# Binarised convolution on one core: products into an unused bank, planes released one by one, row sums moved

## What is computed

```
v  = group_norm(x, 32 groups)                # per image and group of 8 channels
xn = batch_norm(v) * gamma + beta            # statistics over all images
t  = +1 where xn > 0, -1 otherwise           # sign
xc = clip(xn, -1, 1)
y  = conv3x3(t, conv_w) + conv_b             # 256 -> 256 channels, pad 1
b_sum = conv3x3_of_ones(sum over channels of xc * t) + beta_b
b_cnt = conv3x3_of_ones(256)                         + beta_b
out = x + y * (b_sum / b_cnt)
```

## Time and profile before

| | |
|---|---|
| median of 3 runs | 935.04 us (934.71 to 936.57) |
| the profiled execution, its own time | 934.54 us |
| its span, first to last instruction | 932.7 us |
| PE busy | 782.7 us (84%) |
| DVE busy | 779.0 us (84%) |
| ACT busy | 600.6 us (64%) |
| mean granted TensorE clock | 0.931 of full |

### The profile page before, as it was taken

One profiled execution on the slowest core, in us unless ns is written; L12 is line 12 of the kernel. 1 busy time (PEld: TensorE's weight loads), 2 busy tenths in 40 slices (PEclk: granted clock), 3 DMA queues, 4 the chain that ended last, 5 costly groups with the idle time before them and its releaser, 6 DMA issues. The chain is left out here.

```text
span 932.7 us, 12739 instructions
## 1 busy us (share of the span) xinstructions
PE 782.7 (84%) x4686; PEld 464.9 (50%) x4686; DVE 779.0 (84%) x1217; ACT 600.6 (64%) x490; POOL 141.4 (15%) x160
## 2 busy tenths in 40 slices
PE   2100005999999999999999999999999999999996
PEld 2100003555555555555555555555555555555553
DVE  4999888899888888888888979797879787979755
ACT  2042636868777777777777777777768686868310
POOL 0089400011111111111011111111111111101011
PEclk9655556999999999999999999999999999999998
DMA  9999972369888888888887869696969696958489
GB/s 358 430 405 379 419 325 81 135 180 286 256 243 229 250 227 248 229 237 248 220 266 202 288 174 315 166 316 159 312 168 303 172 291 188 290 157 215 131 214 269
DMA packets 43478, 232.79 MB, mean 250 GB/s; under 512 B 10560, under 2 KB 10688, under 8 KB 39360
## 3 DMA queue, kind: packets, MB, share of 16 engines
q0 software_dynamic: 18144, 101.16, 42.1%
q1 hardware_dynamic: 24544, 131.25, 38.7%
q10 hardware_dynamic: 768, 0.12, 0.1%
HBM read 180.73 MB, written 51.79 MB: 249 GB/s over the span
## 5 line engine op out<-in xcount | busy, mean ns | idle before, releaser
L606 PE MATMUL acc<-V,U 128*128 128x385 f16 (+1 forms) x4608 | 769.4, 330 | 11.8 <-DVE V L832 10.1
L606 PEld LDWEIGHTS acc<-V,U 128*128 128x128 f16 x4608 | 451.0, 98 | 325.6 <-issue 12.8
L477 ACT ACTIVATE sn<-acc,inv_s 128x784 f32<-128x784 f32 x128 | 116.9, 913 | 206.8 <-PE acc L606 200.9
L350 POOL DMA_DIRECT2D y<-x x63 | 53.9, 856 | 724.6 <-DVE y L919 711.4
L919 DVE SCALAR_TENSOR_TENSOR y<-y,vec,bmap 128x1568 f32<-128x1568 f32 (+1 forms) x65 | 117.6, 1810 | 0.2
L455 ACT ACTIVATE r<-xb,ab 128x1568 f32<-128x1568 f32 x64 | 106.6, 1690 | 6.3 <-ACT u L430 4.0
L430 ACT ACTIVATE u<-xb,ab 128x1624 f16<-128x1624 f32 x63 | 109.0, 1732 | 0.2
L440 ACT ACTIVATE T<-u 128x1680 f16<-128x1680 f16 x60 | 95.6, 1594 | 2.2 <-DVE D L826 2.2
L443 ACT ACTIVATE T<-T 128x1568 f16<-128x1568 f16 x58 | 87.6, 1511 | 1.8
L579 PE MATMUL csum<-mv,cst 128*128 128x32 f32 x2 | 0.6, 397 | 90.7 <-DVE mv L690 90.7
L826 DVE TENSOR_TENSOR D<-T 128x1568 f16<-128x1568 f16 x63 | 61.3, 973 | 15.3 <-ACT T L443 15.0
(11 more groups left out here) (110 smaller groups left out, 414.8 us busy)
## 6 DMA issues: line engine op xcount, KB each, us to landing
xb<-x SPq DMA_DIRECT2D x64, 812.0 KB, 6.5
y<-x POOLq DMA_DIRECT2D x63, 784.0 KB, 8.0
out<-y POOLq DMA_DIRECT2D x63, 784.0 KB, 9.3
y<-x SPq DMA_DIRECT2D x16, 1568.0 KB, 8.7
bmap<-map_rows SPq DMA_DIRECT2D x32, 784.0 KB, 6.4
xb<-x SPq DMA_DIRECT2D x14, 1568.0 KB, 10.2
V<-w_t SPq DMA_DIRECT2D x2, 1152.0 KB, 14.7
out<-y SPq DMA_DIRECT2D x2, 392.0 KB, 3.0
```

Source lines behind the costliest of these rows:

```text
L477: nc.scalar.activation(sn[:, b, half], acc[:, b, :, 0:N], ACT.Copy, scale=inv_s[:, b:b + 1])\
L606: last = nc.tensor.matmul(by_row(acc[:, g % 2, bank, 0:N])[:, :, lo:hi], U[:, ci, digits, k, dx, co * P:(co + 1) * P], by_row(V[:, a, ci, ...
```

## The change

Six edits:

1. PE: after the group sums, 36 matmuls of 128 x 392 into `box` (`keep_busy`): 26 as soon as `w_pool` and `scale_ready` allow, 10 after the wait for the coefficients.
2. DVE: groups 0 and 1 of image 0 go through `first_group`: each of the two FIRST planes is made as soon as its half of D is there, the odd one first, as an instruction of 392 elements with its own `v_first`.
3. PE: FIRST of group (0, 0) waits per plane and part (`v_first` 1 to 4), bank 1 first.
4. ACT makes the `T` of group 1 (into `T01`, memory of `y`) after `sign(0, 0, 1)`; DVE made it before. `snapshot(0, 0, 0)` now stands ahead of `sign(0, 0, 3)`, and `snapshot(0, 0, 1)` ahead of `complement(0, 1)`.
5. SP: image 0 uses the usual order, so `crow_load(0)` stands ahead of all loads of image 2.
6. DVE: `beta_map(1)` moves behind `finish(0, 2)`.

The core of the diff:

```diff
+WARM = (26, 10)
+        early = y[:, 0:2].rearrange("p g f -> p (g f)").bitcast(F16).rearrange("p (r w) -> p r w", w=W)
+        T01 = early[:, 0:66]
...
             for g in range(G4):
                 first_load(g)
-            load(0, x_rows[2], 0)
-            load(0, x_rows[2], 1)
             sp.wait_ge(zeros_in, 16)
-            crow_load(0)
-            map_store(0)
-            map_load(0, 0)
-            map_load(0, 1)
-            load(0, x_rows[2], 2)
-            load(0, x_rows[2], 3)
+            image(0, x_rows[2])
...
             sign(0, 0, 1)
+            act.wait_ge(u_ready, 1)
+            act.wait_ge(t_ready, 1)
+            nc.scalar.activation(T01[:, 30:60], u[:, 1, 0:HR + 2], ACT.Relu, scale=2.0).then_inc(t_ready, 1)
             sign(0, 0, 2)
             absolute(0, 0, 0)
             absolute(0, 0, 1)
             complement(0, 0)
+            snapshot(0, 0, 0)
             sign(0, 0, 3)
-            snapshot(0, 0, 0)
             absolute(0, 0, 2)
             absolute(0, 0, 3)
+            snapshot(0, 0, 1)
             complement(0, 1)
-            snapshot(0, 0, 1)
...
+            def keep_busy(count):
+                for _ in range(count):
+                    nc.tensor.matmul(box[:, 0:N], U[:, 0, 0, 0, 0, 0:P],
+                                     U[:, 0, 0, 0].rearrange("p b o -> p (b o)")[:, 0:N], start=True, stop=True)
+            pe.wait_ge(w_pool, WP * CT)
+            pe.wait_ge(scale_ready, 2)
+            keep_busy(WARM[0])
...
                 for part in range(CT if by_channels else 1):
-                    if by_channels:
-                        pe.wait_ge(v_first, part + 1)
-                    for bank in banks:
+                    for bank in banks[::-1] if by_channels else banks:
                         k = planes[bank]
+                        if by_channels:
+                            pe.wait_ge(v_first, 2 * part + 2 - bank)
...
-            pe.wait_ge(w_pool, WP * CT)
+            keep_busy(WARM[1])
             first(0, 0, 0, by_channels=True)
...
+            def first_group(g, t, d):
+                at_least(dve, cq_done, g)
...
+                dve.wait_ge(t_ready, g + 1)
+                nc.vector.tensor_scalar(t[:, 1:28:2], t[:, 31:58:2], 2.0, None, ALU.mult).then_inc(t4_ready, 1)
+                dve.wait_ge(t4_ready, g + 1)
+                nc.vector.tensor_tensor(rows(d[:, 1], 1), pair(3), pair(1), ALU.subtract).then_inc(aq_done, 1)
+                dve.wait_ge(aq_done, g + 1)
+                nc.vector.tensor_tensor(plane(1), d[:, 1, 2:HR:4], d[:, 1, 1:HR:4], ALU.add).then_inc(v_first, 1)
+                nc.vector.tensor_scalar(T8[:, :], t[:, 30:30 + HR], 4.0, 3.0, ALU.mult, ALU.subtract)\
+                  .then_inc(t8_ready, 1)
+                dve.wait_ge(t8_ready, g + 1)
+                nc.vector.tensor_tensor(d[:, 0], t[:, 32:32 + HR], T8[:, :], ALU.subtract).then_inc(cq_done, 1)
+                dve.wait_ge(cq_done, g + 1)
+                nc.vector.tensor_tensor(plane(0), d[:, 0, 2:HR:4], d[:, 0, 1:HR:4], ALU.add).then_inc(v_first, 1)
...
-            differences(0, 0, D00)
-            first_planes(0, 0, 0, D00).then_inc(v_first, 1)
-            differences(0, 1, D)
-            first_planes(0, 0, 1, D).then_inc(v_first, 1)
+            first_group(0, T, D00)
+            first_group(1, T01, D)
...
-            beta_map(1)
...
-            def proceed(n, a):
+            def proceed(n, a, map_after=False):
...
                     finish(*before(g, 3))
+                    if map_after and g == 1:
+                        beta_map(n)
...
-            proceed(1, 1)
+            proceed(1, 1, map_after=True)
```

More of the change, by code:

```diff
@@ L804, in v_planes @@
                 return V[:, a, g % 2, first:first + step + 1:step, g // 2].rearrange("p k (q w) -> p k q w", w=W)
+            def first_group(g, t, d):
+                at_least(dve, cq_done, g)
+                pair = lambda at: t[:, at:at + 62].rearrange("p (j r) w -> p j r w", j=2)[:, :, 0:28:4]
+                plane = lambda j: V[:, 0, g, 2 + 2 * j, 0].rearrange("p (q w) -> p q w", w=W)
+                if g == 0:
+                    dve.wait_ge(u0_ready, 1)
+                    nc.vector.tensor_scalar(t[:, 30:60], u[:, 0, 0:HR + 2], 0.0, 2.0, ALU.max, ALU.mult)\
+                      .then_inc(t_ready, 1)
+                dve.wait_ge(t_ready, g + 1)
[10 more added lines that the diff above has]
+                nc.vector.tensor_tensor(plane(0), d[:, 0, 2:HR:4], d[:, 0, 1:HR:4], ALU.add).then_inc(v_first, 1)
             def differences(m, g, d):
@@ L811, in differences @@
                 if isinstance(m, int) and m == 0:
[L812 to L815, removed]
+                    dve.wait_ge(u_ready, s)
                     nc.vector.tensor_scalar(T[:, 30:60], u[:, g % 2, h:h + HR + 2], 0.0, 2.0, ALU.max, ALU.mult)\
```

## The result

| | before | changed | ratio |
|---|---|---|---|
| median of 11 runs each | 934.71 us (933.60 to 936.92) | 932.50 us (931.67 to 933.17) | 0.9973, 95% interval 0.9965 to 0.9981 |
| the profiled execution | 934.54 us, span 932.7 | 932.56 us, span 930.4 | |

What follows compares the result with a forecast made beforehand. PE bounds the loop, its restart at 223.83 set by the later of PE's and DVE's chains. PE's 0.90 - 0.2 + 0.66 + 0.56 = 1.9 us off 934.54 gives 932.6, plus 0.50 for the median 933.1; range 932.5 to 933.8, chance 0.58.

Steps and rivals of the forecast that it cites:

- DVE's chain: DVE from `beta_map(0)` on: no 2.80 us wait for the row sums, so 2.7 us (2.4 to 3.1) earlier.
- PE's chain: PE from its first product to the restart at 223.83: 1.9 us earlier, the smaller of the two chains.
- the 0.2% line: Least difference told from no change, 1.87 us, so 933.17 is the bound; faster 0.47, same 0.47.
- The 0.50 that I added for the median: Median of the runs taken as 0.50 above the profiled execution, giving 933.1 from 932.6.
- The 24 products: PE's first 24 products in image 0: done at 157.05 instead of 157.95, so PE is 0.90 us ahead.
- The new wait for `ends` of (0, 0): PE ahead of FIRST of group (0, 2), near 173: gives back 0.2 us (0 to 0.4).
- The two old waits: PE's stops at 202.70 (for a `fold`) and 223.83 (`ends` of (1, 0)): both gone, 0.66 + 0.56 us gained.
- Sum on PE: PE's gain at the restart after 223.83: 0.90 - 0.2 + 0.66 + 0.56 = 1.9 us.
- The end: PE's last wait, 1.0 us at the very end; the forecast sum has no term for it.
- The 36 matmuls: PE from 142.40, ahead of the first products: lift the clock after 2.9 us, end at 149.8, cost nothing.
- the broken start: Rival: clock falls among PE's 18 products from 149.8 to 156.05; gain about 0.6, 934.4; chance 0.13.
- DVE stayed late: Rival: small store stays slow or DVE's gain is lost, restart at 223.83 stays; 935.0, in part 934; chance 0.15.

Runs made afterwards that it cites:

- front_only: Edits 1 to 4 alone: the changed kernel with the order of the row sums and of beta_map(1) put back; median 933.80 us, ratio to before 0.9973 to 0.9993.
- rows_only: The kernel before with only the new order of the row sums and of beta_map(1) (edits 5 and 6); median 934.17 us, ratio 0.9983 to 1.0.
- warm_rows: The kernel before with edits 1, 5 and 6 (36 matmuls, new order), planes and T as before; median 933.09 us, ratio 0.9969 to 0.9987.
- before_again: The kernel before, unchanged, run once for a second trace; no median, product 408 at 77.03 us from the start of stage 2 against 76.23 in the first trace.

## Why the store lands sooner: left open

In both traces of before a 16 KB fetch of PE's instructions (0.96 and 1.16 us on a transfer queue of its own) falls at 34.8 or 35.3 us from the start of stage 2, among the two loads and the store; in front_only the 36 matmuls move it to 26.7. Small matmuls in stage 1, where PE is idle, move the fetches alone:

```diff
             last.then_inc(scale_ready, 1)
+            for _ in range(36):
+                nc.tensor.matmul(csum[:, 100:101], mxb[0:1, 0:P], one[:, :], start=True, stop=True)
```

> The kernel before with 36 matmuls of one element in stage 1, where PE is idle for 90 us, into an unused column. They cost no time and do not touch the clock at the first products; they move PE's instruction stream on by 36 matmuls, so each 16 KB fetch comes 6 us earlier, the one at 34.8 us behind the start of stage 2 at about 28.8, ahead of the two loads. Theory (the fetch on the same transfer engines is what made the store of the row sums land 1 us later): the store lands 6.0 us after its issue instead of 7.0, PE restarts at product 408 1.0 us earlier, time 933.9. Rival (the fetch has nothing to do with it): 7.0 us and 934.9.

> front_only with 80 matmuls of one element in stage 1, as in before_shift. The fetches then fall at about 13.4 and 35.4 us behind the start of stage 2, the second of them between the two loads and the store again. Theory (the fetch): the store lands 7.0 us after its issue, restart at 76.0 to 76.3 us, time 934.8, no gain against before, although PE starts 1.5 us earlier. Rival (edits 2 to 4 bring the 1 us): 6.0 us and 933.8.

> front_only with 36 matmuls of one element in stage 1, as in before_shift. One fetch of PE's instructions then falls at about 35 us behind the start of stage 2, between the two loads and the landing of the row sums (31.5 to 38.6 in before). Theory (the fetch costs the store 1 us, and DVE's chain sets PE's restart): the store lands 6.9 to 7.0 us after its issue, restart at product 408 at 76.0 to 76.3 us, time 934.8, so no gain against before, although PE starts 1.5 us earlier. Rival (edits 2 to 4 bring the 1 us): 5.8 to 6.0 us, restart at 75.0 to 75.3, 933.5.

before_shift had its fetches at 20.3 and 41.2, a store of 5.82 us and a restart at 75.22, as the theory says. Its median was 933.73, 1.5 below the 935.23 of before on the same chip, but with one run of 940.2 the interval is 0.9979 to 1.0009, so this is not told from no change. front_shift missed its aim: with 80 the fetches fell at 20.8 and 41.1, so it is one more trace without a fetch beside the store (5.75 us; median 933.38). front_fetch put one at 34.9, and the store landed after 5.06 us:

```profile
179.59 0.40 SPq L231 DMA_DIRECT2D sum_rows<-cs  x1
184.66 0.33 SPq L235 DMA_DIRECT2D crow<-sum_rows  x1
```

Its median was 933.59, like front_only. So a fetch at that time does not always cost the store 1 us, and the theory as I put it falls. I had overlooked, though, that the traces with the new order speak for a part of it: the store took 1.38 to 1.40 us in the nine with no fetch beside it, but 2.55 in rows_only and 2.18 in no_warm, the two where a fetch fell next to it (33.4 against a store issued at 33.0, and 31.4 against 31.5). SP in no_warm:

```profile
178.70 0.40 SPq L231 DMA_DIRECT2D sum_rows<-cs  x1
180.89 0.33 SPq L235 DMA_DIRECT2D crow<-sum_rows  x1
```

The store of image 1 shows no such cost: 3.25 us in no_warm with a fetch beside it, 3.28 in the changed kernel without. What makes the store land sooner is open.

## The clock, the planes, the T

**no_warm** (`WARM = (0, 0)`) and **warm_long** (`WARM = (26, 30)`):

> The changed kernel without the 36 matmuls into the unused bank. The first products begin at about 151.0 us at the half clock. Theory: DVE delivers the four parts 1.9, 1.3 and 1.9 us apart, and six products at the half clock take 1.96, so the half clock is mostly hidden in pauses; what is lost is the part that still lies behind 156.0 us, when the last six begin: 0 to 1 us, depending on when the level rises. I expect it 0 to 0.9 us slower than the changed kernel, so 932.5 to 933.4. Rival (the clock is what the change gains): slower by the 1.5 us that 9 products at the half clock cost, or more, 934.0.

> The changed kernel with 20 more matmuls into the unused bank behind the coefficients (26 and 30 instead of 26 and 10). They take 20 x 0.166 = 3.3 us at the full clock and end at about 154.2 us, past the first three planes, so the 24 first products end at about 158.2 instead of 157.0. Theory (PE's chain is the later one by now): 1.2 us later there, less the wait of 0.2 us at product 120 that it covers, so 1.0 us slower than the changed kernel, 933.5. Rival (DVE's chain still decides): no change against the changed kernel.

Without the 36 matmuls the median is 0.6 higher, 933.08, in the expected range. In its trace the half clock lasted until 155.65, and product 24 was only 0.45 later, since PE's pauses for DVE hid the rest; the runs spread over 3.5 us instead of 1.5. With 20 more: no change (932.43), where I expected 1.0. In the trace the extra matmuls held PE until 152.63 and the 24 products then ran without one pause (PE):

```profile
141.07 11.73 PE L589 MATMUL box<-U 128*128 128x392 f16 x56
152.63 24.08 PE L615 MATMUL acc<-V,U 128*128 128x392 f16 x144
```

Product 24 came 0.7 us later from the start of stage 2 than in the changed kernel, 4583 0.5 later. That is the theory's direction at half the size; the medians of 7 and 11 runs do not show it, so the expected 1.0 was a miss.

**t_on_vector**, the second T made by DVE and not by ACT:

```diff
+                else:
+                    dve.wait_ge(u_ready, g)
+                    nc.vector.tensor_scalar(t[:, 30:60], u[:, 1, 0:HR + 2], 0.0, 2.0, ALU.max, ALU.mult)\
+                      .then_inc(t_ready, 1)
```

> The changed kernel with the T of group 1 made by DVE again (the first half of edit 4 undone). DVE gets one more step of 0.6 us ahead of group 1, so the third and fourth plane come 0.6 us later, the 24 products end 0.6 later, and DVE is later by 0.6 at every place behind. PE: 0.6 later at product 24, and the wait at 120 stays 0.2. Theory (PE's chain is the later one): 0.6 us slower than the changed kernel, 933.1. Rival (ACT's Relu held back ACT and DVE as much as it saved): no change.

Measured 0.63 later at product 24, 0.62 at 4583, median 0.8 higher. As expected: PE's chain is now the later one, and DVE's steps ahead of the fourth plane are on it.

**map_back**, `beta_map(1)` ahead of `finish(0, 2)` again:

> The changed kernel with beta_map(1) back ahead of finish(0, 2) (edit 6 undone). Theory: both orders have the same work ahead of ends(1, 0), so PE's restart and the fold are not moved, and the map of image 1 is not needed for 10 us: no change against the changed kernel, 932.5. Rival: DVE now waits for the rows of sums, since it comes there 2.7 us earlier than before, and 0.3 to 1 us is lost.

Its trace is the changed kernel's at every product. The median is 1.0 higher, though before was 0.5 higher on this chip too, and the runs reach from 931.8 to 934.7. Their spans lie in two groups of five, 929.6 to 930.9 us and 931.8 to 932.4; those of the changed kernel reach from 929.7 to 931.4. One trace of a kernel with this old place, front_fetch, shows what can happen in some executions: the rows of image 1 landed late, DVE waited for them, and PE with it.

```profile
214.93 0.35 DVE L911 TENSOR_REDUCE vsum<-crow 56x58 f32<-56x174 f32 x1 [1.96 <-DMA crow<-sum_rows]
```

```profile
224.45 25.74 PE L624 MATMUL acc<-V,U 128*128 128x392 f16 x144 [2.53 <-DVE y L944]
```

That execution took 937.02, against a median of 933.59. With edit 6, `finish(0, 2)` and its 1.8 us would stand ahead of this wait of 1.96, so it can be cover for a late transfer and is not free of effect as I had written. That it is this that widens map_back's runs is argued, not shown: its one trace has no such wait.

## Further on: the fold and the end

**fold_later**, **split_last**, **pad_vector** and **combined**:

```diff
             pair_sum(0, 0)
-            fold(0, 0)
             transform(0, 0, 2)
             mid(0, 0)
             transform(0, 0, 3)
             ends(0, 0)
+            fold(0, 0)
```

```diff
...
-            snapshot(NI - 1, 3, 1)
+            act.wait_ge(half_done, 1)
+            act.wait_ge(mid_done, 4 * NI - 2)
+            nc.scalar.activation(sn[:, 1, 1, 0], acc[:, 1, 0, 0:N], ACT.Copy, scale=inv_s[:, 1:2]).then_inc(half_snap, 1)
+            act.wait_ge(second_done, 4 * NI)
+            nc.scalar.activation(sn[:, 1, 1, 1], acc[:, 1, 1, 0:N], ACT.Copy, scale=inv_s[:, 1:2]).then_inc(snap2, 1)
...
```

> The changed kernel with two moves on DVE: in group 1 of image 0 T8 is made ahead of the odd plane (an independent step in a place where DVE waits for its own result), and fold(0, 0) behind ends(0, 0). Theory: the last plane comes 0.25 us earlier, the 24 products end 0.17 earlier, and the wait of 0.2 us at product 120 is gone since ends(0, 0) comes 1.8 us earlier. Together 0.35 us less than the changed kernel, 932.1 to 932.2. Rival: the fold now makes quarter_sums of image 0 wait, 0 or slower.

> The changed kernel with the last copy out of PSUM split by bank: ACT copies bank 0 of SECOND of the last group while PE multiplies into bank 1, and THIRD of the last group waits per bank. PE's only wait of the loop, 1.2 us at product 4584, goes. Theory (at the end the later of two chains decides too): the last products end 1.17 us earlier, but POOL's chain of x added to the group before and stored is not moved and ended 2 us ahead of the last store; the two last stores of 392 KB follow DVE. So between 0.5 and 1.2 us less, 931.3 to 932.0. Rival (DMA bound at the end): no change.

> The changed kernel with one more DVE instruction in stage 1, a fill of one unused column. Theory (DVE stands still for 0.36 us ahead of its first half of the last finish for want of instructions, and where it does so is a matter of how many instructions stand ahead: 0.45 us of idle time there in the traces of the changed kernel, front_only, no_warm, warm_long, fold_later and split_last, but 0.09 in those of before, rows_only, warm_rows and t_on_vector): the idle time ahead of L947 near the end goes from 0.45 to 0.09, and a gap of this kind shows ahead of a sum over r instead, where DVE has time. 0.3 us less than the changed kernel, 932.2. Rival (the gap is a wait for a transfer): it stays, no change.

> The changed kernel with the split copy of the last group, T8 ahead of the odd plane in group 1, and the extra fill of pad_vector; the fold stays where it was. Theory: PE 0.17 earlier at product 24 and 0.25 at 120, 1.17 at the end, DVE another 0.36 at the end; the transfers at the end give back a part, as in split_last, where the last additions came 1.12 us earlier and the last store in the trace not at all. Between 0.8 and 1.4 us less than the changed kernel, 931.1 to 931.7. Rival (the end is bound by transfers): as split_last, 931.9.

fold_later: product 24 0.25 earlier and the wait at 120 gone, 0.44 ahead there; then `quarter_sums` waited for the fold, and 0.09 was left. The rival was right. The weight loads of fold_later:

```profile
176.65 0.25 PEld L600 LDWEIGHTS csum<-cst,quarter 128*98 128x98 f32 x2 [0.51 <-DVE quarter L900]
```

split_last: PE's last wait is gone, and the last addition starts at 925.42 instead of 926.54. The span stayed (930.5), the median of 6 runs is 931.89, 0.6 below the changed kernel's. What came between is, I think, POOL's store of the group before: it was issued at 924.43, beside SP's first one at 924.46, where in the changed kernel 1.8 us lay between the two. pad_vector: the 0.45 us of idle time ahead of L947 went to 0.09 as expected, but neither the median (932.43) nor the time from the start of stage 2 to the end moved (782.8 us in its trace, 782.9 in the changed kernel's). combined: 931.98 (931.18 to 932.33, 6 runs, ratio to before 0.9955 to 0.9979), above its expected range and not told apart from split_last (0.9956 to 0.9981). Both beat the kernel before; against the changed one they are 0.5 to 0.6 us lower in the median, which their intervals do not tell from none. So work taken off PE and DVE at the end is mostly lost there, and that transfers bind it is argued from the issue times.

## The prediction, point by point

The time of 932.50 lies in the range, 0.6 below the forecast of 933.1. I gave 0.47 each to faster and to no change, because the forecast lay on the 0.2% line; it came out 0.27% faster. **The step that failed is the price of PE's two old waits in the sum of PE's chain: 1.22 us in the forecast, 1.90 in the traces.** The mechanism held: both chains came earlier, and PE's was the later one.

That the profiled execution took 932.56 where I had 932.6 is luck. PE gained 2.6 us and not 1.9; the end gave 0.36 of it back, and the time outside the span was 0.3 longer (2.1 us for 1.8). The 0.50 that I added for the median came from 3 runs of before and was not there: over 11 runs the median of before lies 0.17 above its profiled execution, that of the changed kernel 0.06 below.

- *The 24 products*: 0.90 worked out, 0.88 measured (157.03 for product 24 against 157.91). The chain of planes was right within 0.05.
- *The new wait for `ends` of (0, 0)*: 0.2 worked out, 0.20 measured: product 120 starts 0.37 behind 119 instead of 0.17. It is in no list of waits, see below.
- *The two old waits*: **this term was mis-sized.** I took 0.66 + 0.56 = 1.22 from the idle times of the earlier trace rows. They were worth 1.90. From 177.96 to 202.89 before passed 24.93 us, for the same work after from 177.27 to 201.31 24.04: 0.89. From 202.89 to 223.83 passed 20.94 for 120 products; after, 288 products took 249.15 - 201.31 = 47.84, so 120 take 19.93: 1.01. PE's idle time begins at the modelled end of a product, 0.33 behind its start, while the next could have started 0.17 behind it. From start to start the two waits were 0.90 and 0.73 long, 0.24 and 0.17 more than listed. A third of 0.26 for `ends` of (0, 3) is in no list, since only 0.10 of it lies behind the modelled end; I carried it on inside the 20.38 us of the earlier trace rows.
- *Sum on PE*: 0.88 - 0.20 + 1.90 = 2.58; measured 920.30 - 917.71 = 2.59.
- *DVE's chain*: 2.7 worked out, 223.69 to 220.92 = 2.77 measured at `ends` of (1, 0); the wait of 0.4 for PE ahead of `ends` of (0, 2) was 0.43. It was not the later chain, as forecast.
- *The end*: I took it as fixed. DVE stood still for 0.36 us more ahead of its last `finish`, "issue" in the trace; so 2.59 became 2.23 at the last addition (926.54 for 928.77), and 2.3 in the span. pad_vector moved the gap away without gain.
- *The 36 matmuls*: forecast to end at 149.8; the clock rose at 147.9 and not from about 145 on, 5.7 us behind their start and not 2.9, so they ended at 150.94, just ahead of the first product at 150.98. It fitted by less than 0.1 us, and that is luck too.
- *Rivals*: the clock did not fall in the broken start: it was granted at 1.00 from 150 to 160 us, through pauses of 0.3 to 0.9 us. The Trainium skill ("TensorE: Matmul & The Clock Gate", section "A second HAM failure mode: psum-queue depth-cycling") reports a clock that swings with small idle times between groups of matmuls; this trace does not show it at three such pauses. DVE stayed late only in front_only, where it took the lead as the rival said.
- *What I had at nothing*: the length of the half clock and the landing of the store differ from run to run, and in before both are in DVE's chain, since a late PE delays the issue of the store too (before_again, 0.8 us at product 408). That is why rows_only and front_only gained 0.7 and 1.1 and not 1.9 and 0: neither half meets fixed conditions.

## What to carry to other kernels

When an engine's wait is to be removed, price it from start to start against the same stretch without the wait, not by the idle time shown. When two chains meet, ask whether one feeds the other, and for each how it varies from run to run: removing the variation of one alone gives a part of what removing both gives. A small transfer that others wait for belongs ahead of the large ones in its queue (5.1 to 7.0 us behind two of them here, 1.4 to 2.6 ahead of them).

## What the runs showed of the hardware

- The full clock came 2.9, 3.2, 4.4, 5.0 and 5.8 us behind the first product in the five traces with cold first products (before, before_shift, before_again, no_warm, rows_only), and between 2.6 and 5.7 behind the start of the extra matmuls where they were there.
- A pause of 2.7 us brought the clock down: in front_fetch the product that could have started at 221.75 started at 224.45, the level was half from 224.44, and rose again 3.4 us later, at a cost of 1.7 us for 10 products. Two stretches of that trace (us, PE, PEld, DVE, ACT, POOL, clock, DMA, GB/s):

```profile
226.00:227.00 1.00, 1.00 (x4) 0.45 (x3) 1.00 (x2) 0.00 (x0) 0.00 (x0) 0.50 1.00 275
228.00:228.50 0.50, 0.50 (x5) 0.29 (x4) 0.50 (x1) 0.00 (x0) 0.44 (x1) 1.00 0.84 320
```

- One more DVE instruction far ahead moved a gap of 0.36 us ("issue") on DVE from one place to another: in the changed kernel it stood ahead of the last `finish`, in pad_vector, as in before, ahead of a sum over `r`, where DVE has time. Its cause is not shown.
